# The expert layer of a graph and attention network: from all rows through every expert to 34 parts of 128 routed rows

## The reference

```python
def _L0_ffn_ref(x, router_w, w1, b1, w2, b2):
    E, C, F, K = (8, 768, 384, 2)
    logits = flat @ router_w.T
    probs = jax.nn.softmax(logits.astype(jnp.float32), axis=-1)
    top_w, top_i = jax.lax.top_k(probs, K)
    top_w = (top_w / top_w.sum(-1, keepdims=True)).astype(x.dtype)
    out = jnp.zeros_like(flat)
    for e in range(E):
        w_e = jnp.sum(top_w * (top_i == e), axis=-1)[:, None]
        h = jax.nn.gelu(flat @ w1[e] + b1[e], approximate=False)
        out = out + w_e * (h @ w2[e] + b2[e])
    return out.reshape(B, T, Cc)
...
x = x + _L0_ffn_ref(_layernorm(x, axis=-1)[None], ...)[0]
```

## Time and profile before

| | us |
|---|---|
| median of 3 runs | 3585.93 (3583.48 to 3592.32) |
| profiled execution, whole | 3583.17 |
| its span, first to last instruction | 3581.5 |
| TensorE busy | 2892.7 (81%) |
| VectorE busy | 2028.6 (57%) |
| ScalarE busy | 1270.8 (35%) |
| GpSimd busy | 265.5 (7%) |
| mean granted clock of TensorE | 0.899 |

### The profile page before, as it was taken

The page is one execution under the profiler, slowest core; times in us unless marked ns, Lnnn a source line. Parts: engine busy times, 40 slices in busy tenths (PEclk is TensorE's granted clock), DMA queues, the critical chain, the costliest instruction groups (busy, mean ns, idle before and its releaser), DMA issues. The chain is left out here.

```text
span 3581.5 us, 42656 instructions
## 1 busy us (share of the span) xinstructions
PE 2892.7 (81%) x15884; PEld 2540.3 (71%) x15885; DVE 2028.6 (57%) x2844; ACT 1270.8 (35%) x1928; POOL 265.5 (7%) x232
## 2 busy tenths in 40 slices
PE   6664887877877859969999986968798699799777
PEld 5553677876877858938888973746666576788776
DVE  6654477877877832253333342363299355688754
ACT  1222275565665521121112110022199101566520
POOL 1332030030030000000000001000000000111100
PEclk9988898988988979979999996978899698899988
DMA  0012111111111172101010022013454120443223
GB/s 29 14 29 50 47 36 59 36 47 59 36 47 59 38 175 52 39 4 51 26 53 26 26 69 53 0 44 120 140 128 88 45 87 0 94 101 76 46 61 91
DMA packets 83081, 204.39 MB, mean 57 GB/s; under 512 B 9866, under 2 KB 39164, under 8 KB 81700
## 3 DMA queue, kind: packets, MB, share of 16 engines
q1 hardware_dynamic: 82950, 202.56, 21.2%
HBM read 153.80 MB, written 44.89 MB: 55 GB/s over the span
## 5 line engine op out<-in xcount | busy, mean ns | idle before, releaser
L831 PE MATMUL ps<-h,e_gat_aggregate 125*125 125x193 f32 x2400 | 408.3, 333 | 90.0 <-DVE e_gat_aggregate L815 73.9
L831 PEld LDWEIGHTS ps<-h,e_gat_aggregate 125*125 125x125 f32 x2400 | 401.8, 192 | 96.8 <-DVE e_gat_aggregate L815 77.8
L103 PE MATMUL ps<-w_pair_experts,hidden_experts 128*125 128x384 f32 x1440 | 257.6, 338 | 5.3 <-DVE x L1237 3.5
L103 PE MATMUL ps<-ln_turned,w_pair_experts 128*128 128x512 f32 (+1 forms) x1296 | 252.0, 356 | 9.4 <-DVE w_pair_experts L1221 9.4
L103 PEld LDWEIGHTS ps<-w_pair_experts,hidden_experts 128*125 128x125 f32 x1440 | 250.7, 185 | 10.5 <-DVE x L1237 6.2
L103 PEld LDWEIGHTS ps<-ln_turned,w_pair_experts 128*128 128x128 f32 x1296 | 212.0, 190 | 50.7 <-DVE w_pair_experts L1221 12.2
L103 PE MATMUL ps<-gat_w_pair_gat_scores,x_turned 128*125 128x384 f32 x1080 | 199.0, 348 | 39.1 <-DVE gat_w_pair_gat_scores L689 38.6
L103 PEld LDWEIGHTS ps<-gat_w_pair_gat_scores,x_turned 128*125 128x125 f32 x1080 | 197.2, 193 | 40.7 <-DVE gat_w_pair_gat_scores L689 39.3
L813 DVE TENSOR_TENSOR e_gat_aggregate<-e_gat_aggregate 125x1250 f32<-125x1250 f32 x120 | 175.2, 1460 | 87.4 <-DMA gat_bias_gat_aggregate<-in_gat_b 48.5
L314 PE MATMUL ps<-dst_hot_build_adjacency,src_hot_build_adjacency 125*125 125x128 bf16 x2380 | 186.1, 235 | 43.4 <-DVE dst_hot_build_adjacency L267 42.4
L777 ACT ACTIVATE e_gat_aggregate<-row_gat_aggregate,from_src 125x1250 f32<-125x1250 f32 x120 | 160.7, 1339 | 166.9 <-PE ps L831 139.3
(11 more groups left out here) (312 smaller groups left out, 4895.4 us busy)
## 6 DMA issues: line engine op xcount, KB each, us to landing
stock<-in_moe_w SPq DMA_DIRECT2D x16, 1152.0 KB, 6.3
row_gat_aggregate<-r_scratch SPq DMA_DIRECT2D x24, 625.0 KB, 6.5
V_home<-q_scratch SPq DMA_DIRECT2D x48, 312.5 KB, 6.5
rows_dense_rows_from<-node_scratch SPq DMA_DIRECT2D x10, 1080.0 KB
stock<-in_gat_w SPq DMA_DIRECT2D x4, 2304.0 KB, 8.5
q_scratch<-V_home SPq DMA_DIRECT2D x6, 1250.0 KB, 4.5
k_scratch<-V_home SPq DMA_DIRECT2D x6, 1250.0 KB, 4.5
V_home<-k_scratch SPq DMA_DIRECT2D x24, 312.5 KB, 6.3
```

What stands on the lines that cost most here:

```text
L103: last = pe.matmul(out, left(x), right(y), start=start and n == 0, stop=stop and n == 2)
L831: last = pe.matmul(ps[0:TP, bank(head, d // 2), d % 2 * (C + 1):(d % 2 + 1) * (C + 1)], e[:, n % 3, 0, d * TP:(d + 1) * TP], h[:, t, head, :],
```

## The change

The experts no longer compute on all rows. `route` builds lists on the chip: for each of the 2500 pairs of row and chosen expert a slot, with the slots of one expert together and each expert's region rounded up to 256 slots. There are always 17 loads of 256 slots (`LOADS`), each with one expert's weights, and 34 parts of 128 (`PARTS`). A slot's row number goes to `slot_token`, its weight to `slot_gate`, the expert of each load to `load_expert`. They are found by counting matmuls, running sums of small vector instructions, and 20 rounds (10 tiles x 2 choices) that add up one-hot products on TensorE. Slots that stay empty point at 128 spare rows behind the 1250.

The layernorm before `route` also stores its normalized rows to a DRAM tensor, `token_scratch`; a ring buffer is written again only when its store has landed. In `experts`, x with the b2 biases goes to `sum_scratch`. For each part GpSimd loads 128 rows by an indirect DMA (four buffers), TensorE turns them around, and up and down products run with the rows as the stationary side and 384 columns of weights moving; the hidden part is transposed in between. ScalarE scales the result by the slots' weights into `y` (three buffers), and GpSimd adds it to `sum_scratch` by an indirect adding store, which waits for the one before to have landed. Weights are split once per load, 17 times instead of 8, into two buffers. ScalarE's and VectorE's programs are written out for the 34 parts, without a loop. The layernorm behind reads x from `sum_scratch`. The first expert's weights are no longer loaded ahead.

```diff
...
+            if rows_to is not None:
+                for t in range(NT):
+                    sp.wait_ge(normed_ready, t + 1)
+                    move_rows(sp, rows_to[t * TP:(t + 1) * TP, :], normed[:, t % 3, :], row_stored[t % 3])
+                for n in range(3):
+                    sp.wait_ge(row_stored[n], 32 * ((NT + 2 - n) // 3))
...
+                        if rows_to is not None:
+                            v.wait_ge(row_stored[t % 3], 32 * (t // 3))
...
+PART = 128
+PER_LOAD = 2
+LOADS = (2 * N + EXPERTS * (PER_LOAD * PART - 1)) // (PER_LOAD * PART)
+PARTS = LOADS * PER_LOAD
...
+            marks = either[:].rearrange("p t e -> p (t e)")
+            pe.matmul(ps[0:TP, 4, 0:NT * EXPERTS], before[:], marks, start=True, stop=True)
+            pe.matmul(ps[0:TP, 5, 0:NT * EXPERTS], all_ones[:], marks, start=True, stop=True).then_inc(counted, 1)
+            for n in range(2 * NT):
+                pe.wait_ge(hot_ready, n + 1)
+                last = pe.matmul(ps[0:PART, 6, 0:3 * PARTS], row_hot[:, n % 2, :], part_hot[:, n % 2].rearrange("p k s -> p (k s)"),
+                                 start=n == 0, stop=n == 2 * NT - 1)
+                last.then_inc(placed, 1)
...
+            for c in range(2):
+                v.tensor_scalar(chosen[:, c], rank[:], float(c), None, ALU.is_equal)
+            step(v.tensor_scalar(either[:], rank[:], 1.5, None, ALU.is_lt))
+            v.sem_inc(chosen_ready, 1)
...
+            for t in range(NT):
+                step(v.tensor_tensor(start[:, t + 1, :], start[:, t, :], totals[:, t, :], ALU.add))
...
+                v.tensor_scalar(row_hot[:, n % 2, :], row_iota[:], row_of[:, c, t:t + 1], None, ALU.is_equal)
+                v.tensor_scalar(part_hot[:, n % 2, 0], part_iota[:], here, token[:, t:t + 1], ALU.is_equal, ALU.mult)
+                v.tensor_scalar(part_hot[:, n % 2, 1], part_iota[:], here, gate[:, c, t:t + 1], ALU.is_equal, ALU.mult)
+                step(v.tensor_scalar(part_hot[:, n % 2, 2], part_iota[:], here, None, ALU.is_equal))
+                v.sem_inc(hot_ready, 1)
+            v.wait_ge(placed, 2 * NT)
...
+            def load(n):
+                e = sp.value_load(load_expert[0:1, n:n + 1], min_val=0, max_val=EXPERTS - 1)
+                if n >= 1:
                 sp.dma_start(w1, i["moe_w1"][bass.ds(e, 1)].rearrange("a (k p) f -> p (a k) f", p=128)).then_inc(w1_in, 16)
-                sp.wait_ge(w2_split, e + 1)
+                if n >= 2:
+                    sp.wait_ge(bias_added, PER_LOAD * (n - 1))
+                sp.dma_start(b1[:, n % 2, :], i["moe_b1"][bass.ds(e, 1), :].partition_broadcast(128)).then_inc(b1_in[n % 2], 16)
+                if n >= 1:
...
+            load(0)
+            for t in range(NT):
+                sp.wait_ge(b2_added, 2 * t + 2)
+                move_rows(sp, sum_scratch[t * TP:(t + 1) * TP, :], x[:, t, :], x_stored)
+            for n in range(1, LOADS):
+                load(n)
...
+            pool.wait_ge(spare_stored, 32)
+
+            def fetch(n):
+                if n >= 4:
+                    pool.wait_ge(row_turned, n - 3)
+                pool.indirect_dma_start(out=rows[:, n % 4, :], out_offset=None, in_=token_scratch[:, :],
+                                        in_offset=bass.IndirectOffsetOnAxis(ap=slot_token[:, n:n + 1], axis=0)).then_inc(row_in[n % 4], 16)
+
+            for n in range(3):
+                fetch(n)
+            for n in range(PARTS):
+                if n + 3 < PARTS:
+                    fetch(n + 3)
+                pool.wait_ge(y_ready, 2 * n + 2)
+                if n == 0:
+                    pool.wait_ge(x_stored, 32 * NT)
+                if n >= 1:
+                    pool.wait_ge(y_added, 16 * n)
+                pool.indirect_dma_start(out=sum_scratch[:, :], out_offset=bass.IndirectOffsetOnAxis(ap=slot_token[:, n:n + 1], axis=0),
+                                        in_=y[:, n % 3, :], in_offset=None, compute_op=ALU.add).then_inc(y_added, 16)
+            pool.wait_ge(y_added, 16 * PARTS)
...
+                for k in range(KD):
+                    last = pe.transpose(ps[:, k // 4, k % 4 * PART:(k % 4 + 1) * PART], rows[:, n % 4, k * 128:(k + 1) * 128], ident[:])
+                last.then_inc(row_turned, 1)
...
+                pe.wait_ge(gelu_done, n + 1)
+                if n >= 1:
+                    pe.wait_ge(h_split, n)
+                for k in range(KF):
+                    last = pe.transpose(ps[:, TURN, k * PART:(k + 1) * PART], hidden[:, n % 2, k * 128:(k + 1) * 128], ident[:])
+                last.then_inc(h_turned, 1)
...
+                for j in range(2):
+                    if n >= 1:
+                        pe.wait_ge(y_ready, 2 * (n - 1) + j + 1)
+                    for k in range(KF):
+                        last = product(pe, ps[:, DOWN + j, 0:384], lambda a: hidden_T[:, n % 2, a, k, :],
+                                       lambda c: w2_pair[:, load % 2, c, k, j * 384:(j + 1) * 384], k == 0, k == KF - 1)
+                    last.then_inc(down_done, 1)
...
+            turn(0)
+            turn(1)
+            pe.wait_ge(b2_added, 2 * NT)
+            for n in range(PARTS):
+                up(n)
+                if n >= 1:
+                    down(n - 1)
+                turn_hidden(n)
+                if n + 2 < PARTS:
+                    turn(n + 2)
...
+            def leave(n):
+                if n >= 3:
+                    a.wait_ge(y_added, 16 * (n - 2))
+                for j in range(2):
+                    a.wait_ge(down_done, 2 * n + j + 1)
+                    a.activation(y[:, n % 3, j * 384:(j + 1) * 384], ps[:, DOWN + j, 0:384], ACT.Copy,
+                                 scale=slot_gate[:, n:n + 1]).then_inc(y_ready, 1)
...
+            first_layer(0)
+            row_tops(0)
+            row_tops(1)
+            second_layer(0)
+            for n in range(PARTS):
+                gelu(n)
+                if n >= 1:
+                    leave(n - 1)
+                hidden_tops(n)
+                if n + 2 < PARTS:
+                    row_tops(n + 2)
+                after = n // PER_LOAD + 1
+                if after < LOADS:
+                    (first_layer if n % PER_LOAD == 0 else second_layer)(after)
+            leave(PARTS - 1)
...
+                add_bias(n)
+                hidden_rest(n)
+                if n + 2 < PARTS:
+                    row_rest(n + 2)
+                after = n // PER_LOAD + 1
+                if after < LOADS:
+                    (first_layer if n % PER_LOAD == 0 else second_layer)(after)
...
-        expert_weights = [(i["moe_w1"][0], 0), (i["moe_w2"][0], KD * FF)]
-        dense_rows_from(nc, g, node_scratch, 18, i["gat_w"][3 * D:6 * D], i["b_out"], True, x, x_in=i["x"], ahead=expert_weights)
+        dense_rows_from(nc, g, node_scratch, 18, i["gat_w"][3 * D:6 * D], i["b_out"], True, x, x_in=i["x"])
...
+            with nc.sbuf_tensor("ln1_turned", [128, 2, KD, N], F32R) as turned:
+                g["xT"] = turned
+                layernorm_turned(nc, g, x, g["xT"], stats_there=True, rows_to=token_scratch)
+                route(nc, g, i)
+            experts(nc, g, i, x, token_scratch, sum_scratch, ahead=[(i["q_w"], 0)])
...
-            layernorm_turned(nc, g, x, g["xT"], later=[
+            layernorm_turned(nc, g, x, g["xT"], x_in=sum_scratch, later=[
...
```

312 lines of the change are left out of this document (207 added, 105 removed).

## The result

The changed kernel takes **3392.55 us** (median of 4 runs, 3387.87 to 3396.28) against 3585.94 (4 runs of before beside it): ratio 0.9457, 95% interval 0.944 to 0.9474. That is 193 us less, 23 less than the forecast of 3415, and inside the range. The profiled execution took 3393.07 us, its span is 3391.3, its mean granted clock 0.885 (before 0.899).

A forecast was written before the change was run, and what follows sets the result against it. Experts was taken as bound by the number of TensorE matmul columns. Experts -218, route +25, layernorm before +3, layernorm after +19 make -171: 3583.2 to 3412, forecast 3415 us with the runs' median 2.8 higher, range 3380 to 3514.

The forecast's parts named there:

- The part: In experts, one of 34 parts of 128 rows was forecast at 8.4 us, 285.6 us in all.
- store chain: In experts, each adding store waits for the last to land: issue 2 plus flight 5.8, 7.8 us a part (5 to 13.7).
- DMA engines 7.0: In experts, weights, bias row, row fetch and adding store take 7.0 us of DMA engine time a part (5.9 to 8.8).
- The ring: In experts, dependent ScalarE, VectorE and TensorE work from one bias to the next, through weight rests: 7.4 us a part.
- The step that failed: In GpSimd's queue, the next row fetch stands behind the waiting store; TensorE was said to need it three parts later.
- Four limits don't interlock without loss: In experts, TensorE with waits 7.8, ring 7.4, store chain 7.8 and DMA engines 7.0 together were taken as 8.4 us.
- The stall of 5: At the start of experts, 10.5 MB of queued DMA delays the second weight pair: 5 us (0 to 15).
- Stores and DMA at 9.2 to 12 us a part: Rival in experts: stores and DMA set the pace; at 10.2 us a part +61 us, 3476; chance 0.26.
- Table loads: Rival on ScalarE in experts: alternating Gelu and Copy reload tables, a part of 10 us, 3469; chance 0.03.
- The clock: Rival on TensorE in experts: a mean clock of 0.85 makes a part 9.3 us, +31, 3446; chance 0.10.
- GpSimd held beside VectorE: Rival in experts: VectorE's weight rests delay GpSimd's issues, up to 2.8 us a part, 10.6 in all, 3490; chance 0.08.
- the sign that was set for the rival: If stores pace experts, idle before gated results or row transposes is put to DMA or GpSimd, TensorE under 75% busy.

The follow-up runs named there:

- e1: Changed kernel with rows fetched four parts ahead instead of three, each fetch queued before the store instead of behind it: 3391.62 us, ratio 0.9447.
- e10: Changed kernel with odd parts adding into a second DRAM tensor (two store chains) and rows fetched four ahead, before the store: 3365.44 us, ratio 0.9381.
- e9: Changed kernel with odd parts adding into a second DRAM tensor, so a store waits only for the last but one: 3396.37 us, ratio 0.9471.
- e3: Changed kernel with each part's indirect store plain instead of adding, so the sum over experts is left out: 3374.22 us, ratio 0.9403.
- e2: Changed kernel with 16 of the 17 loads of weight pairs left out, all parts using the first expert's weights: 3381.28 us, ratio 0.9417.
- e4: Kernel before plus only the layernorm's row stores and route's slot lists, which its experts don't use: 3617.68 us, ratio 1.0081.
- e8: Changed kernel with the splitting of weights left out from the third load on, all loads still transferred: 3430.39 us, ratio 0.9573.
- e7: Changed kernel with 16 of 17 weight-pair loads left out and plain stores instead of adding ones: 3365.44 us, ratio 0.9385.
- e12: Changed kernel with one store chain, rows fetched four ahead before the store, and 16 of 17 weight-pair loads left out: 3372.07 us, ratio 0.9401.
- e5: Kernel before with the first expert's weights loaded at the start of experts instead of ahead during dense_rows_from: 3576.30 us, ratio 0.9975.

## Why the prediction came out as it did

Point by point, with its own terms; the total was 23 us too high.

- *The part*, 8.4 us forecast, 7.98 measured: 34 x 0.42 = 14 us of the difference. Three of the limits were sized well: TensorE's own 7.3 (7.23 where nothing waits), store chain 7.8 (7.86 in the lines above, and 8.0 in e1, where it holds), DMA engines 7.0 (0.92 x 7.98 = 7.3, and 0.96 x 7.21 = 6.9 in e10). The 0.5 us that TensorE was given for its usual waits isn't there: in e10 it is busy 99%. The store chain came out right from two wrong terms: the issues of a part take 1.59 + 0.99 = 2.6 us instead of 2, but a fetch's issue lies beside the flight, and a store lands 6.4 us after its issue begins. The ring (7.4) was too long: it hides in 7.23. That 8.4 came as near as 0.42 us is partly luck: it was a judgement on how four limits would add, and the loop that held TensorE most isn't among them.
- *The step that failed* is "behind that waiting instruction in its queue stands the next row fetch, for which TensorE's transposes wait, three parts later". It is one part later: when the fetch for part n+3 is let go, by the `y` of part n-1, TensorE is through up product n and down product n-1, and it transposes the rows of n+3 one round on. With the 8.02 us from those transposes to the store two parts on that made a loop of some 8 us a part, the one that does hold TensorE (18.9 us). e9 and e10 against e1 show it. The forecast named only the chain, and its rule "34 us for each microsecond" of a store fails with it: in e3 a store lands 1.3 us sooner and the time falls by 18 us, not 44.
- *Four limits don't interlock without loss*: right, but the loss was 0.75 us over TensorE's 7.23 and not 1.1, and it comes from the fetch loop and the chain, on flights that a full DMA makes long, and not from the ring.
- *Start*: first up product at +26.3 (25.8 forecast, though its terms, 20.6 + 2.9 + 1.0 + 0.9, make 25.4). The stall of 5 behind the queued DMAs didn't come: the second part's up product follows 6.95 us after the first, the third 7.26 after that.
- *End*: 15.6 us from the last down product to the next stage, forecast 9.3. The last store itself was sized right, 5.5 us from its issue to its landing at 1920.95. What was left out is ahead of it and behind it. It is issued at 1915.41, 3.7 us after its `y` (1911.17 + 0.58), because it waits for the store before; and the next stage begins 2.4 us after it has landed. The chain was late because the store of 1900.41 lands only at 1908.40, SP having issued the 2.36 MB of q_w for a later stage at 1897.89: 8.0 us after its issue. In e2, which has no other load of weights in the stage's middle, the store beside q_w takes 8.0 us too and all others 5.4 to 6.0.
- *`route`*: +29.7 and +30.5 (e4), forecast 25 in 18 to 33. The mis-sized term is the round, 1.00 instead of 0.75: 5 us.
- *Layernorms*: +0.3 before `route`, forecast 3 in 0 to 8; the stores keep up. +19.0 after, as forecast.
- *"The weights no longer loaded ahead free nothing that it waits for: 0"*: wrong. The stage waits for its rows 6 us longer with them (before 49.9, e4 50.5, against 43.6 and 43.8). I had looked at its matmuls and not at what its first tiles wait for.
- *Rivals.* Stores and DMA at 9.2 to 12 us a part: no, though e8 shows how near it was, 8.82 from a shift of one load. Table loads: one in the stage, as forecast. The clock: 1.00. GpSimd held beside VectorE: the fetch's issue takes 982 to 1002 ns in all 30 cases between 1640 and 1905 us, and VectorE's weight rests run beside 19 of them; beside the store's issue (1567 to 1642) none runs, so that one isn't tested. The Trainium skill (SBUF — State Buffer, Who interferes with whom) has an instruction with two SBUF inputs contend with one of GpSimd that reads SBUF, but the same section also reports that `tensor_tensor`, which the rests are, wasn't seen to stall a DMA; these 19 issues agree with that, and the prediction had used the first half alone. The Trainium skill's estimate for a transfer from GpSimd (DMA: Bandwidth & Descriptors, Anatomy of one DMA), 2.9 us here, is short: a fetch in the changed kernel takes 4.9 to 7.6 us from the start of its issue, and 3.9 in the median of e7, where the DMA engines carry least; only e7's plain store, at 3.0, comes near it.
- *What would show it*: the 1224 matmuls and 306 transposes are there, and TensorE is busy 92%. But the sign that was set for the rival came too: the idle time before the row transposes is put down to DMA. It is small, not absent.

The sum again, measured less forecast, in the profiled execution: part -14.2, start -4.5, end +6.3, and -1.6 because the stage before ends 1.66 us later by the mark used here, together -14.0 for `experts`; `route` +4.7; the layernorm before it -2.7; the stages ahead of that -5.3, of which 3.2 in `dense_rows_from`; elsewhere -1.8: -19.1. The median lies 0.5 us below the profiled execution, where I had added 2.8: -22.4.

## What to carry to other kernels

Where several queues feed one engine, write out for each transfer whose result lets it be issued and how many periods later it is wanted: a prefetch that stands behind an instruction which waits for the newest result is one period deep, whatever the number of buffers. Follow the way from there back to the next such issue as well, and divide by the number of periods that it takes. When two loops have nearly the same length, loosening one shows no gain and proves nothing; loosen both before calling either harmless. And a transfer moved ahead "for free" is paid by the transfers beside it: look at what the stage that hosts it waits for.

## What the runs showed that I had not expected

- DMA engines at 0.96 of the time with TensorE at 99% (e10): a nearly full DMA costs nothing where the waits on it have slack, although a fetch then takes 6.7 us instead of 3.9 (e7) and an adding store 7.4 instead of 5.6 (e12).
- An indirect adding store of 128 rows of 3 KB takes GpSimd 1.59 us to issue, a plain indirect one 0.99 (e3) and an indirect load 0.99. Beside the same weight loads it lands in 6.4 us, the plain one in 5.1.
- Taking work off two engines made the kernel 38 us slower (e8), with a 1.15 MB load moved from 4 us behind a row fetch to 0.7 us ahead of one.
- 2.36 MB loaded ahead in a stage that seemed bound by TensorE cost that stage 6 us and the kernel 10 (e5).
